# Twelve transformer layers on one core: a new order of the work items, another place where the loop is cut, and other counts of filling matmuls

## The reference, cut to what matters

```python
for i in range(NL):
    xn = _adaln(x, noise_emb, n1_w[i], n1_b[i])
    qkv = xn @ qkv_w[i].T
    q, k, v = jnp.split(qkv, 3, axis=-1)
    q = _rope(q.reshape(B, L, H, HD))
    k = _rope(k.reshape(B, L, H, HD))
    a = _attn(q, k, v, src_mask).reshape(B, L, D) @ so_w[i].T
    x = x + a
    xn = _adaln(x, noise_emb, n2_w[i], n2_b[i])
    q = _rope((xn @ cq_w[i].T).reshape(B, L, H, HD))
    k = _rope((context @ ck_w[i].T).reshape(B, LC, H, HD))
    v = (context @ cv_w[i].T).reshape(B, LC, H, HD)
    a = _attn(q, k, v, ctx_mask).reshape(B, L, D) @ co_w[i].T
    x = x + a
    xn = _adaln(x, noise_emb, n3_w[i], n3_b[i])
    h = jax.nn.gelu(xn @ f1_w[i].T + f1_b[i], approximate=False)
    x = x + (h @ f2_w[i].T + f2_b[i])
```

## Time and profile before

| | |
|---|---|
| median of three runs | 3621.6 us (3615.82 to 3632.56) |
| the profiled execution | 3622.48 us, span 3620.5 us |
| mean granted TensorE clock | 0.927 |
| PE busy | 3008.7 us (83%) |
| DVE busy | 1981.1 us (55%) |
| ACT busy | 1896.7 us (52%) |
| POOL busy | 806.2 us (22%) |

### The profile page before, as it was taken

One profiled execution on the slowest core, in us unless ns is written; L12 is line 12 of the kernel. 1 busy time (PEld: TensorE's weight loads), 2 busy tenths in 40 slices (PEclk: granted clock), 3 DMA queues, 4 the chain that ended last, 5 costly groups with the idle time before them and its releaser, 6 DMA issues.

```text
span 3620.5 us, 50670 instructions
## 1 busy us (share of the span) xinstructions
PE 3008.7 (83%) x15727; PEld 1040.6 (29%) x15727; DVE 1981.1 (55%) x3535; ACT 1896.7 (52%) x2677; POOL 806.2 (22%) x1327
## 2 busy tenths in 40 slices
PE   7899999968888788888878846888888887888866
PEld 2463333222222222222222211222222222222225
DVE  4324444248475583756648366658375574746524
ACT  5432333327656474665747534647566474665632
POOL 0003444522212122122222102212212222212211
PEclk9999999979999899998999977989999899999987
DMA  1100000001010111101011001011110111101030
GB/s 41 53 18 7 1 1 1 10 20 39 26 42 25 30 41 33 36 27 42 27 32 46 22 8 43 22 33 40 35 36 27 36 32 32 42 21 50 24 116 7
DMA packets 125569, 110.70 MB, mean 31 GB/s; under 512 B 49983, under 2 KB 116077, under 8 KB 125293
## 3 DMA queue, kind: packets, MB, share of 16 engines
q1 hardware_dynamic: 114924, 97.80, 9.1%
q10 hardware_dynamic: 10368, 9.44, 0.8%
HBM read 41.96 MB, written 0.52 MB: 12 GB/s over the span
## 4 chain that ended last, share of the span: by engine, by line
PE 65%; DVE 15%; issue 6%; ACT 6%; POOL 4%; SPq 2%; DMA 1%; ACTq 0%; DVEq 0%; POOLq 0%
PE ps L516 11%; DVE arena L793 7%; PE ps L461 6%; PE ps L490 4%; PE ps L641 3%; PE ps L626 3%; PE ps L583 3%; PE ps L1462 3%; PE ps L1478 3%; ACT arena L666 3%; PE ps L545 2%; PE ps L569 2%; PE ps L533 2%; PE ps L524 2%; PE ps L561 2%
## 5 line engine op out<-in xcount | busy, mean ns | idle before, releaser
L666 ACT ACTIVATE arena<-ps 128x1024 f32<-128x1024 f32 x960 | 936.4, 1023 | 341.5 <-PE ps L490 338.0
L793 DVE TENSOR_REDUCE arena<-ps 128x1 f32<-128x512 f32 x1536 | 966.6, 684 | 215.0 <-PE ps L461 204.6
L516 PE MATMUL ps<-arena 128*32 128x512 f32 x3840 | 512.9, 609 | 20.5 <-ACT arena L666 18.0
L461 PE MATMUL ps<-arena 49*128 49x512 bf16 x1536 | 318.4, 411 | 239.5 <-DVE arena L793 192.0
L490 PE MATMUL ps<-arena 52*128 52x512 bf16 x1920 | 346.5, 387 | 28.2 <-ACT arena L666 24.9
L795 DVE TENSOR_REDUCE arena<-ps 128x3 f32<-128x462 f32 (+1 forms) x576 | 303.6, 579 | 95.2 <-PE ps L468 91.4
L875 POOL TENSOR_TENSOR arena<-arena,zeros 128x16 bf16<-128x16 f32 x192 | 42.3, 220 | 1055.9 <-DVE arena L793 624.6
L461 PEld LDWEIGHTS ps<-arena 49*128 49x128 bf16 x1536 | 75.2, 94 | 585.3 <-DVE arena L793 477.8
L885 POOL TENSOR_TENSOR arena<-arena 128x512 f32<-128x512 f32 x96 | 122.0, 1271 | 454.8 <-ACT arena L698 454.8
L891 POOL TENSOR_TENSOR arena<-arena 128x512 bf16<-128x512 f32 (+1 forms) x84 | 92.5, 1101 | 547.6 <-ACT arena L725 547.6
L804 DVE TENSOR_TENSOR h<-ps,h 128x512 f32<-128x512 f32 x48 | 33.2, 691 | 294.6 <-PE ps L545 294.6
(11 more groups left out here) (381 smaller groups left out, 4297.6 us busy)
## 6 DMA issues: line engine op xcount, KB each, us to landing
arena<-arena SPq DMA_DIRECT2D x720, 64.0 KB
arena<-we_dram SPq DMA_DIRECT2D x24, 578.5 KB, 8.0
arena<-arena ACTq DMA_DIRECT2D x144, 64.0 KB
w<-weights_dram SPq DMA_DIRECT2D x26, 320.0 KB, 3.0
w<-weights_dram SPq DMA_DIRECT2D x13, 512.0 KB, 3.7
arena<-arena SPq DMA_DIRECT2D x384, 6.0 KB
arena<-arena SPq DMA_DIRECT2D x288, 19.2 KB
w<-weights_dram SPq DMA_DIRECT2D x39, 128.0 KB, 2.1
```

What stands on the lines that cost most here:

```text
L461: pe.matmul(s_bank(slot + r), qst[b][rows, idx, P * qt:P * (qt + 1)], kst[b][rows, idx, :], start=True, stop=True).then_inc(s_full, 1 + (z ...
L516: mm = pe.matmul(bank(7)[32 * j:32 * j + 32, :], v, prob[:, slot, j, :], start=(g % 2 == 0 and kt == 0), stop=(a == 0 and g % 2 == 1 and k ...
L666: act.activation(prob[:, chunk_no(b, a, g, kt) % NPROB, 2 * p:2 * p + 2, :], e_bank(slot).rearrange("p (j n) -> p j n", j=2), ACT.Exp, sca ...
L793: op = ve.tensor_reduce(nmax[:, g % 2, r, n:n + 1], s_bank(slot + r), AX.X, ALU.max, negate=True)
```

## The change

All places of the table are new. Most items keep their neighbours on their engine; what changes is

- the whole pattern is shifted, so that score.0.0.0.0 has place 7. The pv of the last group, both pvt, evac, sel, inv and out of batch element 1's cross attention stand at 371 to 377 and so belong to the head of the next turn of the loop (in `post` for the last layer). The last item of a turn is then pv.1.1.2.0 on PE, st.0.1.0 (six DMAs) on ACT, proj.0.1 on DVE, and hi.0.1 on POOL;
- some neighbours on PE are exchanged: exp.0.0.1.1.0 goes behind pv.0.0.0.2 and proj.1.0, turn.0.0.2 behind exp.0.0.1.1.2 and pv.0.0.1.1, exp.0.0.2.0.1 ahead of score.0.0.3.6, exp.1.0.1.1.1 ahead of score.1.0.2.6, turn.0.1.0 and turn.0.1.1 one or two items forward, tail.0.0 ahead of pv.0.1.0.0, exp.1.1.3.1.0 ahead of pv.1.1.2.0, pvt.1.0.1 behind two exp, and a few more of this kind;
- on DVE score.0.0.2.4 goes ahead of apply.1.0; on ACT hi.1.0 goes ahead of exp.0.0.1.0.1, turn.0.1.1 ahead of exp.1.0.3.0.1, tail.0.0 ahead of exp.0.1.1.0.0 and evac.1.1.0 behind the two exp of its neighbour group; on SP the loads of the cross, self, n2 and cout weights change places, the last to the head of the turn, ahead of mrow.0.0.0; on POOL ktail goes behind two msplit;
- `FILL` is out.0.1: 4 (was 3), out.1.1: 2 (was 3), f1.0.0: 1 (as before), and new var.1.0: 1. `score` and `center` get the code for fills too, but no item of theirs is in `FILL`. In `var` the fill stands ahead of the wait for the squares.

```diff
-    ('score', 0, 0): [[0, 1, 3, 4, 6, 9, 10, 12], [15, 16, 18, 20, 21, 23, 26, 28], [33, 36, 41, 44, 47, 56, 58,
-        62], [69, 75, 82, 85, 87, 89, 94, 95]],
...
-    ('exp', 1, 1): [[[321], [322]], [[332], [333]], [[346], [347]], [[353], [360]]],
...
-    ('pv', 1, 1): [[329], [339], [359], [361]],
-    ('tail',): [[269, 286], [335, 357]],
-    ('pvt',): [[[277, 278], [289, 290]], [[340, 343], [362, 363]]],
...
-    ('evac', 1): [[200, 259], [344, 367]],
...
-    ('sel', 1): [[206, 264], [349, 368]],
...
-    ('inv', 1): [[210, 265], [352, 369]],
-    ('out',): [[145, 298], [271, 370]],
-    ('center',): [[-45, 157, 302], [38, 285, 373]],
-    ('var',): [[-35, 163, 303], [45, 288, 376]],
-    ('apply',): [[-33, 169, 304], [46, 294, 379]],
-    ('proj',): [[-23, -21, 171, 101], [52, 65, 296]],
-    ('hi',): [[-20, -13, 176, 106], [57, 78, 297]],
-    ('st', 0): [[-17, -16, -15], [-7, -6, -5], [184, 203, 213], [135, 140, 146]],
...
-    ('load',): {'cout': 411, 'cross': 320, 'ffn': 410, 'n0': -127, 'n1': 60, 'n2': 188, 'self': 84, 'sout': 295},
+    ('score', 0, 0): [[7, 8, 10, 11, 13, 16, 17, 19], [21, 23, 26, 29, 30, 32, 34, 37], [42, 45, 48, 50, 53, 65, 66,
+        69], [72, 81, 86, 88, 91, 95, 101, 102]],
...
+    ('exp', 1, 1): [[[327], [329]], [[339], [340]], [[349], [350]], [[363], [366]]],
...
+    ('pv', 1, 1): [[336], [346], [370], [371]],
+    ('tail',): [[274, 294], [343, 364]],
+    ('pvt',): [[[285, 286], [298, 299]], [[348, 351], [372, 373]]],
...
+    ('evac', 1): [[211, 268], [353, 374]],
...
+    ('sel', 1): [[214, 271], [356, 375]],
...
+    ('inv', 1): [[217, 272], [359, 376]],
+    ('out',): [[150, 308], [280, 377]],
+    ('center',): [[-38, 162, 309], [47, 293, 380]],
+    ('var',): [[-27, 168, 310], [51, 296, 383]],
+    ('apply',): [[-17, 175, 311], [55, 297, 386]],
+    ('proj',): [[-16, -9, 177, 107], [58, 71, 303]],
+    ('hi',): [[-14, -6, 181, 112], [60, 84, 304]],
+    ('st', 0): [[-13, -11, -10], [-4, -3, -2], [188, 206, 207], [117, 158, 170]],
...
+    ('load',): {'cout': 398, 'cross': 332, 'ffn': 409, 'n0': -106, 'n1': 63, 'n2': 208, 'self': 151, 'sout': 283},
...
-        FILL = {("out", 0, 1): 3, ("out", 1, 1): 3, ("f1", 0, 0): 1}
+        FILL = {("out", 0, 1): 4, ("out", 1, 1): 2, ("f1", 0, 0): 1, ("var", 1, 0): 1}
...
             def var(it):
                 _, b, k = it
                 slot, at = z.use("e", it)
+                if it in FILL:
+                    pe.wait_ge(e_free, z.room("e", it, 1))
+                    fill(it, e_bank(slot)[:, 0:S])
                 pe.wait_ge(squared, z.after("sq", ("center", b, k), it))
                 pe.wait_ge(e_free, z.room("e", it, 1))
                 pe.matmul(e_bank(slot)[:, 0:S], mean_w, cols(sq, b), start=True, stop=True)\
```

More of the change, by code:

```diff
@@ L92 @@
-    ('msplit', 0, 0): [14, 30, 63, 99],
-    ('msplit', 0, 1): [222, 233, 250, 262],
-    ('msplit', 1, 0): [136, 155, 187, 215],
-    ('msplit', 1, 1): [312, 317, 325, 341],
-    ('turn', 0, 0): [17, 35, 66, 102],
-    ('turn', 0, 1): [230, 242, 260, 266],
-    ('turn', 1, 0): [137, 159, 190, 220],
-    ('turn', 1, 1): [313, 318, 331, 342],
-    ('mrow', 0, 0): [19, 43, 72, 108],
-    ('mrow', 0, 1): [251, 253, 272, 276],
-    ('mrow', 1, 0): [139, 162, 202, 227],
-    ('mrow', 1, 1): [315, 327, 337, 345],
@@ new lines @@
+    ('score', 1, 1): [[312, 314, 315], [318, 319, 320], [325, 328, 331], [335, 337, 342]],
+    ('msplit', 0, 0): [20, 40, 74, 103],
+    ('msplit', 0, 1): [228, 239, 256, 267],
+    ('msplit', 1, 0): [142, 164, 196, 223],
+    ('msplit', 1, 1): [316, 321, 334, 345],
+    ('turn', 0, 0): [24, 44, 76, 108],
+    ('turn', 0, 1): [235, 244, 269, 273],
+    ('turn', 1, 0): [143, 165, 197, 226],
+    ('turn', 1, 1): [322, 324, 338, 347],
+    ('mrow', 0, 0): [28, 52, 82, 109],
+    ('mrow', 0, 1): [252, 263, 275, 276],
@@ new lines @@
+    ('mrow', 1, 0): [149, 178, 203, 231],
+    ('mrow', 1, 1): [326, 330, 341, 352],
+    ('exp', 0, 0): [[[31, 35, 41, 49], [33, 36, 46, 54]], [[56, 64, 70, 79], [59, 67, 73, 80]], [[90, 100, 106,
+        111], [96, 104, 110, 115]], [[121, 125, 129, 134], [123, 126, 131, 135]]],
+    ('exp', 0, 1): [[[261], [270]], [[278], [279]], [[281], [282]], [[288], [289]]],
+    ('exp', 1, 0): [[[152, 156, 161, 173], [154, 157, 167, 174]], [[179, 185, 192, 199], [180, 186, 198, 201]],
+        [[212, 219, 224, 230], [216, 220, 229, 234]], [[240, 245, 249, 254], [241, 246, 251, 258]]],
@@ new lines @@
+    ('evac', 0): [[93, 140], [287, 300]],
+    ('evac', 1): [[211, 268], [353, 374]],
+    ('sel', 0): [[97, 144], [291, 301]],
+    ('sel', 1): [[214, 271], [356, 375]],
+    ('inv', 0): [[99, 145], [292, 302]],
+    ('inv', 1): [[217, 272], [359, 376]],
[4 more added lines that the diff above has]
+    ('proj',): [[-16, -9, 177, 107], [58, 71, 303]],
[3 rows of a table added]
@@ L137 @@
+    ('ktail',): 260,
+    ('vals',): [14, 87, 118],
+    ('f1',): [[313, 317], [389, 393]],
+    ('f2',): [323, 396],
+    ('gain',): [-114, 61, 191],
+    ('biasf',): 213,
+    ('load',): {'cout': 398, 'cross': 332, 'ffn': 409, 'n0': -106, 'n1': 63, 'n2': 208, 'self': 151, 'sout': 283},
 }
@@ L448, in score @@
                 _, b, a, g, n = it
+                if it in FILL:
+                    pe.wait_ge(s_free, z.room("s", it, 2))
+                    fill(it, s_bank(z.use("s", it)[0]))
                 if g == 0 and n == 0:
```

27 lines of the change are left out of this document (6 added, 21 removed), and 2 rows, old and new, of the table PLACES.

## The result

The changed kernel takes 3635.38 us, the median of 14 runs (3621.82 to 3649.45), against 3621.58 for the kernel before in 14 runs on the same chip (3610.14 to 3633.04): a ratio of 1.0037, 95% interval 1.0023 to 1.0051. It is slower by 14 us where no difference was forecast (3620 us). The time lies within the forecast range of 3590 to 3650, but not for the reasons given there. The profiled execution took 3630.46 us around a span of 3628.6 us at a mean granted clock of 0.931, against 3622.48, 3620.5 and 0.927 before.

The account below looks back on a forecast made before the run. No engine was taken as the bound everywhere: layers are one hand-over between PE, DVE and ACT. Terms -6.6 + 0.5 + 8.4 - 3.6 = -1.3; 3622.5 - 1.3 - 0.9 = 3620.3, so 3620 us; range 3590 to 3650.

Parts of the forecast that it names:

- (a): Moved loop cut: branches come earlier, engine orders hardly change; -2.1 and +1.0 us at each of six turns, -6.6 us.
- cheap-branch rival: ACT's branch at the loop turns is cheap, gaining 16 us more, about 3605 us; chance 0.04.
- (b): Two fills instead of three at out.1.1: saves nothing at a high clock, rest counted under (a); 0 us.
- (c): Four fills instead of three at out.0.1: score.1.1.0.0 keeps its time, f1.0.0 may move; +0.5 us, bounds -3 and +10.
- (d): New fill at var.1.0: it ends 0.91 us later, net +0.7 us in each of twelve layers; +8.4 us.
- The swaps: Exchanged neighbours on PE and ACT can fill short waits: -0.3 us a layer, -3.6 us, bounds -7 and +4.
- The slower one: At the turns the clock falls ahead of out.1.1: +4.2 us a turn, +25 us, about 3656 us; chance 0.25.
- the sign of a faster kernel: Edge windows at the turns, sel product to next layer's center product: under 41 us would show the faster rival.

Follow-up runs that it names:

- e1: Changed kernel with proj.0.1 ahead of hi.0.0 in the table, so DVE's last addition of proj.0.1 no longer waits for POOL; 3604.15 us, ratio 0.9951.
- e4: Kernel before with hi.0.0 ahead of proj.0.1 in the table, so DVE's last addition of proj.0.1 waits for POOL; 3660.36 us, ratio 1.0097.
- e7: Kernel before with only the loop's cut moved, to between pv.1.1.2.0 and pv.1.1.3.0; 3610.26 us, ratio 0.9969.
- e13b: e6 with three fills ahead of out.1.1 instead of two; 3597.84 us, ratio 0.9942.
- e9b: e6 with no fill ahead of out.1.1 instead of two; 3639.68 us, ratio 1.0046.
- e10b: e7 with the changed kernel's fills, four at out.0.1 and two at out.1.1; 3601.37 us, ratio 0.9933.
- e8b: e6 with three fills ahead of out.0.1 instead of four; 3614.79 us, ratio 0.9975.
- e6: e1 without the fill ahead of var.1.0; 3597.63 us, ratio 0.9936.
- e3: Changed kernel without the fill ahead of var.1.0; 3632.43 us, ratio 1.0022.
- e8: Kernel before with one fill ahead of var.1.0; 3625.19 us, ratio 1.0009.
- e5: e1 with the loop's cut put back behind out.1.1; 3606.72 us, ratio 0.9955.

## Why the prediction was wrong

**The step that failed** is the sentence of (a) that the order on each engine hardly changes there, and with it the treatment of the whole table as an order. Of proj.0.0, hi.0.0, proj.0.1 and hi.0.1 every engine keeps its order, and so the sum has no term for them. But a place in the table also sets how much of another engine's work a wait asks for. The missing term is +31 us in the changed kernel (after against e1) and +37 in the kernel before (e4). Without it, e1 took 3604 us. The rest of the sum, forecast -1.3 us, came to -17, so the missed term and the gains that were set too low cancel in part. That 3635 lies within 3590 to 3650 is luck.

**(a), the moved cut**, forecast -6.6 us, bounds -13 and +25. Where the branch costs and what it frees were right: ACT's branch lies ahead of the evacuation, and the queue of ACT at the turn shows it 3.4 us from issue to the next instruction (3.3 to 3.9 at the six turns, against the 2.9 of the earlier trace rows):

```profile
L2423 ACTq COMPARE_BRANCH  x1: 50/50/50, 1429.7 to 1429.7; - x1
L2423 ACTq FUSED_REGOPS  x1: 56/56/56, 1433.1 to 1433.1; - x1
```

P costs 3.6 us a turn in e7 (21.4 / 6) and P and S together 3.1, where the prediction had 2.8 + 1.0. What the edges get back was set too low: 5.7 us a turn in E (230.9 to 196.6 for the six turns), not 4.9, and S gives another 3 in all. Measured in the kernel before: -11 us; in the changed kernel -14. By the 108 ns of the Trainium skill (Advanced Engine Details and Errata, Control Flow Timing) the branch would have cost next to nothing. As an estimate from that figure, P would not have risen by 21 us in e7. The trace does not agree: the cheap-branch rival is out on six turns of ACT and of DVE (2.8 to 3.3 us).

**(b)**, a fill less at out.1.1, forecast 0: right, two or three make no difference (e13b). The reason given, that it lies in a wait, was incomplete. The fills lie in a wait and still carry 42 us (e9b).

**(c)**, a fill more at out.0.1, forecast +0.5 us, bounds -3 and +10: from the first fill ahead of out.0.1 to score.1.1.0.0 the twelve layers take 120.7 us before and 123.6 after, so the fill is hidden behind the DMA but for 0.24 us a layer. Its effect on the clock was under-rated: with (b), -9 in the kernel before (e10b against e7), -17 in the new order (e8b against e6).

**(d)**, the fill of var.1.0, forecast +8.4 us. V rises by 13.5 us, past the upper bound of 13; 11 of it are the fill's (after against e3), the rest comes with the order. In the timeline of PE the fill lies directly ahead of var.1.0, and proj.1.0 waits for DVE, where in the earlier trace rows it did not:

```profile
2661.51 1.13 PE L445 MATMUL ps<-consts 128*128 128x512 f32 x2
2662.47 1.02 PE L578 MATMUL ps<-sq,consts 128*128 128x512 f32 x2
...
2666.65 1.98 PE L592 MATMUL ps<-xn,w 128*128 128x512 f32 x4 [0.99 <-DVE xn L825]
```

This wait belongs to the new order and not to the fill. It is 0.76 to 0.99 us long in all twelve layers with the fill (after) and without it (e3), and is missing in all twelve of before and of e8: the exponential product that stood in it went behind proj.1.0, and where (d) says that the wait is then gone, it stays. proj.1.0 starts 6.8 us behind center.1.0 without the fill and 7.6 to 7.7 with it, in the old order and in the new, where (d) had 0.7 us a layer. What the prediction lacked is the clock at out.0.0, which gives V's loss back, and F, which takes part of that again: +3 to +6.5 in all.

**The swaps**, forecast -3.6 us: -4 (e6 against e10b), not told from nothing. So the match with the forecast shows little.

**The rivals.** The slower one (3656 us) put the loss at the turns, in the clock ahead of out.1.1. Its clock mechanism is there, over pv and pvt, but the loss is in every layer that has a next one, and the turns are where the time came back. Their edge windows, 36.9 to 40.4 us, lie under the 41 that was to be the sign of a faster kernel: the sign looked only behind sel.1.1.1, and the loss lies ahead of it. The evacuation came 1.8 us after the end of the value products (0.8 before), not 2.8 later, because these products were late themselves. From before to after the measured steps are: cut -11, counts of out -9, order -4, fill of var.1.0 +6.5, wait +31, together +14. These are steps of one path from kernel to kernel, so they must add up; on another path a step has another size (the cut is worth 2.6 from e5 to e1). The wait is larger than all others; with e1's places the same sum ends at -17.

## What to carry to other kernels

In a kernel whose waits are derived from a common order of items, comparing each engine's own order is not enough: compare the threshold of every wait before and after, because an exchange of two items that no engine sees can put one engine behind another. Where TensorE idles for some 3 us on the critical path, work without a result in that gap can be worth more than the whole order of the items (42 us against 4 here), and it needs a bank that is free when the gap begins. Two gains or losses that lie in the same idle stretch do not add; test them together.
